# Unit 1's projection and silu moved into the preparation, and the order of the waits before VectorE's scan

## The reference

```python
xz = jnp.einsum('blc,ec->ble', xs, in_w)
xi, z = (xz[..., :d_inner], xz[..., d_inner:])
xc = jax.lax.conv_general_dilated(xi.transpose(0, 2, 1), conv_w[:, None, :], ...)
xi = jax.nn.silu((xc + conv_b[None, :, None]).transpose(0, 2, 1))
dbl = jnp.einsum('bld,ed->ble', xi, xp_w)            # dt, B, C
delta = jax.nn.softplus(jnp.einsum('blr,dr->bld', dt, dt_w) + dt_b)
dA = jnp.exp(delta[..., None] * A)
dBu = delta[..., None] * Bm[:, :, None, :] * xi[..., None]
h = dA_t * h + dBu_t                                  # over 1024 places
y = (sum_s h * C + xi * Dp) * jax.nn.silu(z)
out = jnp.einsum('bld,cd->blc', y, out_w)
```

## Time and profile before

| what | value |
|---|---|
| median of three runs | 4428.48 us (4428.17 to 4444.77) |
| profiled execution, its own time | 4430.18 us |
| its span | 4428.3 us |
| TensorE (PE) busy | 3965.8 us, 90% |
| VectorE (DVE) busy | 3394.4 us, 77% |
| ScalarE (ACT) busy | 2923.4 us, 66% |
| GpSimd (POOL) busy | 2383.8 us, 54% |
| mean granted TensorE clock | 0.943 |

### The profile page before, as it was taken

The page is one execution under the profiler, slowest core; times in us unless marked ns, Lnnn a source line. Parts: engine busy times, 40 slices in busy tenths (PEclk is TensorE's granted clock), DMA queues, the critical chain, the costliest instruction groups (busy, mean ns, idle before and its releaser), DMA issues.

```text
span 4428.3 us, 42070 instructions
## 1 busy us (share of the span) xinstructions
PE 3965.8 (90%) x14264; PEld 1457.9 (33%) x14264; DVE 3394.4 (77%) x2997; ACT 2923.4 (66%) x3492; POOL 2383.8 (54%) x1108
## 2 busy tenths in 40 slices
PE   6889987999879998799987999889997899878997
PEld 2332234222342224422243222432234322342223
DVE  1469967799658996599965998669977699658996
ACT  2577747676577675767666775777747677576664
POOL 0137752577416773177732776237752477425773
PEclk9989999999999999899998999989999899997888
DMA  1157651677317763376624674347651677406661
GB/s 42 44 124 189 173 132 44 168 173 185 97 56 176 189 164 85 84 185 168 166 60 120 173 185 126 87 120 186 174 139 44 158 177 181 105 19 169 159 164 43
DMA packets 166830, 579.12 MB, mean 131 GB/s; under 512 B 22572, under 2 KB 23320, under 8 KB 163064
## 3 DMA queue, kind: packets, MB, share of 16 engines
q1 hardware_dynamic: 152280, 538.67, 48.8%
q10 hardware_dynamic: 14336, 37.76, 2.8%
HBM read 467.12 MB, written 71.48 MB: 122 GB/s over the span
## 4 chain that ended last, share of the span: by engine, by line
PE 54%; DVE 24%; ACT 13%; issue 4%; DMA 3%; POOL 1%; SPq 0%; DVEq 0%; ACTq 0%; POOLq 0%
DVE arena L1445 14%; PE ps L769 12%; PE ps L836 8%; PE ps L790 7%; PE ps L691 6%; DVE ps L1440 5%; PE ps L678 3%; PE ps L549 3%; PE ps L609 3%; ACT arena L1137 3%; PE ps L799 2%; PE ps L782 2%; ACT arena L934 2%; DMA arena<-dl 2%; ACT arena L916 2%
## 5 line engine op out<-in xcount | busy, mean ns | idle before, releaser
L1527 POOL TENSOR_TENSOR arena<-arena 128x1024 f32<-128x1024 f32 x768 | 1806.4, 2358 | 902.8 <-DVE arena L1445 897.4
L1445 DVE TENSOR_TENSOR_SCAN arena<-arena,ps 128x1024 f32<-128x1024 f32 x768 | 1756.3, 2287 | 116.2 <-ACT arena L1137 16.4
L1137 ACT ACTIVATE arena<-arena,a_all 128x1024 f32<-128x1024 f32 x768 | 865.2, 1141 | 324.7 <-DVE arena L1445 240.4
L1440 DVE TENSOR_TENSOR ps<-ps,arena 128x1024 f32<-128x1024 f32 x768 | 931.5, 1213 | 165.1 <-PE ps L771 163.6
L769 PE MATMUL ps<-arena,spread 32*128 32x512 f32 x1536 | 894.0, 664 | 100.5 <-DVE arena L1445 91.8
L771 PE MATMUL ps<-arena,spread 32*128 32x512 f32 x1536 | 887.2, 664 | 0.0
L790 PE MATMUL ps<-arena,gather 128*32 128x512 f32 x3072 | 546.0, 656 | 11.8 <-POOL arena L1527 11.8
L836 PE MATMUL ps<-x 96*96 96x512 f32 x1008 | 498.5, 612 | 0.0
L769 PEld LDWEIGHTS ps<-arena,spread 32*128 32x128 f32 x1536 | 233.7, 189 | 739.1 <-issue 424.6
L891 ACT ACT_TABLE_LOAD x234 | 300.2, 1283 | 24.8 <-DMA wo<-in_wo 20.5
L1490 POOL TENSOR_TENSOR x<-x,arena 96x512 f32<-96x512 f32 x64 | 114.0, 1781 | 369.5 <-DVE arena L1310 369.5
(11 more groups left out here) (150 smaller groups left out, 5191.1 us busy)
## 6 DMA issues: line engine op xcount, KB each, us to landing
arena<-dl SPq DMA_DIRECT2D x768, 512.0 KB, 5.2
dl<-arena ACTq DMA_DIRECT2D x64, 384.0 KB, 5.9
x<-pn SPq DMA_DIRECT2D x56, 247.5 KB, 7.0
arena<-in_x SPq DMA_DIRECT2D x9, 1536.0 KB, 13.9
arena<-xq SPq DMA_DIRECT2D x64, 192.0 KB, 5.8
arena<-arena ACTq DMA_DIRECT2D x64, 192.0 KB, 5.3
out<-x SPq DMA_DIRECT2D x64, 192.0 KB, 2.1
arena<-xq SPq DMA_DIRECT2D x64, 191.8 KB, 5.2
```

The lines of the kernel that those rows point to most:

```text
L1137: act.activation(da[:, m % DAS, :], dbc[:, m % DBC, :], ACT.Exp, scale=a_all[:, v // 2, m:m + 1]).then_inc(da_ready, 1)
L1440: dve.tensor_tensor(driven, driven, bmat[:, v % 2, :], ALU.mult).then_inc(bu_ready, 1)
L1445: dve.tensor_tensor_scan(hs[:, m % HSS, :], da[:, m % DAS, :], driven, 0.0, ALU.mult, ALU.add).then_inc(h_ready, 1)
L1527: pool.tensor_tensor(product, product, cmat[:, v % 2, :], ALU.mult).then_inc(pr_ready, 1)
```

## The change

Two things are changed. First, unit 1's input projection moves from slot 0 of unit 0 into TensorE's preparation, behind z of unit 0, and its silu moves from slot 1 into ACT's preparation, behind z's silu, under the same silu table. C of unit 0 moves behind the first broadcast on TensorE, and its copies (`keep_c`) behind the first decay on ACT. u's move is issued ahead of z's silu. The table loads are taken out of `silu_xi` and `silu_z` and written at their calls. Second, VectorE's scan names the wait for its product ahead of the waits for `da_ready` and `y_acc`.

```diff
@@ TensorE, prep_first
                     for c in range(2):
                         gate_in(0, 0, c, 2 + c)
+                    pe.wait_ge(xs_in[1], (p * QUADS + 1) * XSL)
+                    for c in range(2):
+                        pe.wait_ge(delta_ready, 2 * V + c + 1)
+                        project_in(V + 1, 0, 1, c)
+
+                def first():
+
+                    broadcast_u(0, 0)
                     for c in range(2):
                         of_xi(128, c, xp_rep[:, 0, 1, :], 0, c).then_inc(c_ps, 1)
@@ TensorE, prep
-                    if slot == PE_XI:
+                    if slot == PE_XI and v >= 2:
 
                         pe.wait_ge(xs_in[i], (p * QUADS + q + 1) * XSL)
                         pe.wait_ge(c_ready, 2 * V)
-                        if v == 1:
-                            pe.wait_ge(delta_ready, 2 * V)
@@ ACT, early, prep_first, prep, first
                     if slot == ACT_SILU_Z:
+                        act.preload_act_table(ACT.Silu)
                         silu_z(v, 6)
+                        exp_table()
...
+                    act.preload_act_table(ACT.Silu)
                     silu_xi(0)
                     softplus(0)
                     delta_to_rows(0)
                     for c in range(2):
                         keep_b(0, c, 4 + c)
+                    move_u(0)
+                    act.preload_act_table(ACT.Silu)
                     silu_z(0, 2)
-                    move_u(0)
-                    for c in range(2):
-                        keep_c(0, c, c)
+                    silu_xi(1)
+                    exp_table()
...
-                    if slot == ACT_SILU:
+                    if slot == ACT_SILU and v >= 2:
+                        act.preload_act_table(ACT.Silu)
                         silu_xi(v)
                         exp_table()
...
                 def first():
-                    for m in range(DAS - 1):
+                    decay(0, 0)
+                    for c in range(2):
+                        keep_c(0, c, c)
+                    for m in range(1, DAS - 1):
                         decay(0, m)
@@ VectorE, step
+                    dve.wait_ge(bu_ready, n + 1)
                     dve.wait_ge(da_ready, n + 1)
                     if v or m >= HSS:
                         dve.wait_ge(y_acc, V * GPB + (m - HSS) // TRIO + 1)
-                    dve.wait_ge(bu_ready, n + 1)
                     dve.tensor_tensor_scan(hs[:, m % HSS, :], da[:, m % DAS, :], driven, 0.0,
```

More of the change, by code:

```diff
@@ L861, in final @@
                     project(QUADS - 1, 1, 7)
-                scan_stage(prep, lambda: broadcast_u(0, 0), step, conv, final)
+                scan_stage(prep, first, step, conv, final)
                 pe.wait_ge(mo_copied, (p + 1) * 2 * QUADS)
@@ L1029, in silu_xi @@
                     q, i = divmod(v, 2)
-                    act.preload_act_table(ACT.Silu)
                     if v >= 2:
@@ L1047, in silu_z @@
                                        ACT.Silu).then_inc(sz_ready, 1)
-                    exp_table()
                 def softplus(v):
```

## The result

The changed kernel takes 4399.98 us in the median of four runs (4391.17 to 4406.85), beside 4433.54 for the kernel before (4428.17 to 4444.77). The ratio is 0.992, with an interval from 0.9891 to 0.9948. Run once more on another occasion it gave 0.9929 (0.9914 to 0.9944). So it is faster by 0.7 to 0.8%; 4397 was forecast.

What follows compares the result with a forecast made beforehand. TensorE bounds the middle units, VectorE the last unit and most of the last pair. Seven pairs of 4.2 (29.4) plus 7.0 make 36.4 us, less 5 for the clock; from 4430.2 to 4398.8, median 4397, range 4377 to 4418.

Steps and rivals of the forecast that it cites:

- The gap: VectorE, before each scan: idle falls from 129 to 35 ns, 94 ns less per step (bounds 0 and 129 ns).
- Units 1 to 6, 1.2 us a pair: Scan stage, seven pairs with convolution: 1.2 us less, at most TensorE's 1.60 us of idle (bounds 0 and 1.6).
- Unit 7, 1.0 us a pair: Last unit of seven pairs: 12 shorter VectorE steps make 1.1 us, taken as 1.0 (bounds 0 and 1.5).
- Unit 0, 2.0 us a pair: First unit of seven pairs: 1.36 silu wait, 0.1 scans, 0.2 clock, 0.3 end wait; 2.0 us less (bounds 0.7 and 3.3).
- One of my signs of being wrong: Unit 0: the forecast would be wrong if TensorE's granted clock of 0.50 lasts past 288.
- The last pair, 7.0 us: Pair without convolution: 1.5 us less in unit 0 and 5.5 in units 1 to 7 (bounds 0 and 7.9).
- 5 us against, for the clock: Rest of each pair: 5 us lost as the clock's falls and rises move, a third of the 16.6 us run spread.
- The wait order without worth: VectorE's scan: the 129 ns are the product's own completion, only 13 us gained, 4415; chance 0.14.
- The clock eating unit 0's gain: Unit 0: the clock goes down earlier and comes back later, 18 us gained, 4410; chance 0.16.
- More: Unit 0 clock back early, first DMA 0.4 earlier: 1.5 us more per pair, no loss elsewhere, 4378; chance 0.10.
- The late preparation: Preparation: moved projection at 1.2 GHz makes the second product 5.0 us late, 1.1 us slower per pair, 4438; chance 0.05.
- the cover of 0.4 us: Preparation: ACT's exp table is loaded 0.4 us before the first decay's DMA lands, so the moved work costs 0.

Runs made afterwards that it cites:

- the kernels with unit 7 kept busy: Eight extra matmuls, result not used, in unit 7 of every pair: ratio 0.9904 in the changed kernel, 0.9917 with the waits alone, 0.9987 in the kernel before.

## Why the prediction was right, and where only in its sum

- **The gap.** 129 ns to 35 was forecast and measured (34.6 us idle in all). One instruction of 0.05 us in a row and the 35 ns of L1290 were enough. The rule of the Trainium skill (VectorE: DVE Perf Modes, The DRAIN you can't avoid) that a semaphore between two VectorE operations costs nothing extra does not hold, in these runs, for a wait that is an instruction of its own: 129 ns, against 35 where the wait rides on the scan itself. Whether the 35 would be less without any wait no run shows.
- **Units 1 to 6, 1.2 us a pair.** Measured 1.05 in pair 0 (265.37 to 264.32), 1.1 on the mean. TensorE's idle time was the right bound: 81.6 us less in VectorE's gaps, and 55.7 more waiting for TensorE.
- **Unit 7, 1.0 us a pair.** This step failed, in sign. Where the clock allowed, unit 7 took 41.60 and not 42.9 us, 1.3 less. It allowed it in three pairs of seven in each of the two profiles; others took 43.3 to 43.4, and in the first profile two took 49.28 us. The sum over seven pairs is 9.8 us lost and not 7 gained (4.0 lost in the second profile). My words were that a stall on TensorE "eats a little". What was missing was the other half of the row: TensorE busy 36.47 of 42.90 at a mean clock of 0.88 means that the clock is already down for a part of it. The same 118 matmul records took from 41.6 to 50.9 us in these kernels; the old length was not VectorE's alone to set.
- **Unit 0, 2.0 us a pair.** The stretch from the first product did shrink by 1.2 to 3.1 us, but the first product now starts later (projection ahead of the broadcast), as the prediction itself had worked out. From the first scan on it is 1.1 us a pair, between 0.6 and 2.1, and not 2.0: the term was mis-sized. The 1.36 us of the silu wait went, but z started only 0.8 us earlier (275.76 for 276.57): the clock fell earlier (17.1 us at 0.50 for 13.6) and took part of it back, where I had put +0.2. One of my signs of being wrong came with it: the 0.50 lasts past 288, to 288.3.
- **The last pair, 7.0 us.** Measured 13.3 (360.3 to 346.9): 3.2 in unit 0 where I had 1.5, 10.6 in units 1 to 6, 0.5 lost in unit 7. For units 1 to 7 that is 10.1, over my upper bound of 7.9. So it is not only that I took some steps as lost: 72 steps of 94 ns are 6.8 us, and the other 3.8 in units 1 to 6 have another cause. With the move alone the same stretch fell by 2.0 (269.0 to 267.0), with the order of the waits alone by 8.9. The clock there was 0.88 and not 0.86; that it made the difference is not shown.
- **5 us against, for the clock.** The rest of the program was 4.1 us shorter. The term's size had no ground other than the spread of the runs, and no run shows a loss there.
- **The sum.** Together the terms are 36.4, less 5 for the clock 31.4. The profiled spans are 23.2 us apart: 7.8 in units 1 to 6, 7.9 in unit 0, -9.8 in unit 7, 13.3 in the last pair, 4.1 in the rest. The medians are 33.6 apart (4433.54 less 4399.98), in the second series 29.3 (4430.9 less 4401.57); the profiled execution of the changed kernel was 6.9 us slower than its median. So direction and gap were understood, but that the time came within 3 us is luck: unit 7, unit 0 and units 1 to 6 brought 23.5 us less than their terms, the last pair and the rest 15.4 more, and the spread of the executions covers what is left.
- **The rivals.** The wait order without worth: refuted by the kernels with unit 7 kept busy. The clock eating unit 0's gain: half right in kind, and it did so above all in unit 7. More (the clock back early, the first DMA 0.4 us earlier): neither came, the clock rose at 288.3 for 287.6 and the first decay started at 266.72 for 266.51; its sum is 4380 by its own terms (8 x 1.5 and the 5), not 4378. The late preparation: in pair 0 both decays still waited for their DMA, with 0.22 and 0.17 us to spare. But in five of eight pairs ACT's own queue ended the wait for the first decay, which was another sign of being wrong: the cover of 0.4 us was used up there. It cost nothing that shows: from the end of one scan stage to the first scan of the next it is 175.2 us on the mean, 175.8 before.

## What to carry to other kernels

Write the wait that comes last in time first in the code, when the first one written is the one that rides on the instruction: a separate wait instruction behind a VectorE operation costs 68 to 97 ns each time here (gaps of 103 and 132 ns by whether that instruction takes 21 or 50 ns, against 35), and it shows as an EVENT_SEMAPHORE row between the two. Where TensorE is not quite full, a change elsewhere can be paid back by its clock; compare the parts with the clock held before judging them, since an edit that measured 0 alone was worth 0.7% then. A few matmuls for nothing in the gaps (here 12 a pair, some 11 us of TensorE's time by the 3.68 of four such) were worth more than both edits: 1.3%.

## What was not expected of the hardware

The granted clock does not come back at once when TensorE is busy again. In unit 0 it stayed at 0.50 for 17.1 us, in which TensorE was busy 14.86; in unit 7 of pair 1 of the changed kernel the mean over 49.3 us was 0.72 at 44.74 us busy. At half clock TensorE was busier, and that did not bring the clock back at once; why is open.
